# Four-layer image kernel on one Trainium2 core: whole residual tiles in the depthwise layer's transfers, and three setup blocks in another order

## The reference

```python
x = x + _L0_conv_ref(_gn(x), ...)   # attention, 8 heads of 48
x = x + _L1_conv_ref(_gn(x), ...)   # layer norm, diagonal complex state space, gated block
x = x + _L2_conv_ref(_gn(x), ...)   # depthwise convolutions
x = x + _L3_conv_ref(_gn(x), ...)   # RWKV mixing and a full 3x3 convolution

def _L2_conv_ref(x, w77, b77, w53, b53, w35, b35, w7w, w7h, w5w, w5h):
    bias = (b77 + b53 + b35)[None, :, None, None]
    out = dwconv(x, w77, 3, 3) + dwconv(x, w53, 2, 1) + dwconv(x, w35, 1, 2) \
        + dwconv(dwconv(x, w7w, 0, 3), w7h, 3, 0) + dwconv(dwconv(x, w5w, 0, 2), w5h, 2, 0) + bias
    return out
```

## Time and profile before

| | us |
|---|---|
| Median of 3 runs (lowest, highest) | 4443.89 (4439.7, 4444.58) |
| The profiled execution | 4441.98 |
| Its span | 4440.3 |
| Busy in the span: PE, DVE, ACT, POOL | 4000.5, 3117.9, 2279.3, 1358.7 |
| Mean busy share of the DMA engines over the span, largest queue | 21.7% |

### The profile page before, as it was taken

One profiled execution on the slowest core, in us unless ns is written; L12 is line 12 of the kernel. 1 busy time (PEld: TensorE's weight loads), 2 busy tenths in 40 slices (PEclk: granted clock), 3 DMA queues, 4 the chain that ended last, 5 costly groups with the idle time before them and its releaser, 6 DMA issues. The chain is left out here.

```text
span 4440.3 us, 55171 instructions
## 1 busy us (share of the span) xinstructions
PE 4000.5 (90%) x17483; PEld 2387.3 (54%) x17483; DVE 3117.9 (70%) x3175; ACT 2279.3 (51%) x3623; POOL 1358.7 (31%) x1008
## 2 busy tenths in 40 slices
PE   6999999999999999947999998565699999999999
PEld 5777777777777777723444443244244444444444
DVE  4757585757575757557777776425788888879878
ACT  2858585858585858533223332222445545544544
POOL 2858585858575758421111110110300000000000
PEclk8999999999999999968999999788799999999999
DMA  4323232323232323220111100458110110110110
GB/s 130 89 81 102 83 105 83 105 83 105 83 103 80 104 78 110 76 95 15 43 43 60 54 29 29 130 127 267 62 43 0 43 43 0 43 43 0 43 43 14
DMA packets 119503, 317.78 MB, mean 72 GB/s; under 512 B 49744, under 2 KB 51024, under 8 KB 109424
## 3 DMA queue, kind: packets, MB, share of 16 engines
q1 hardware_dynamic: 114000, 294.55, 21.7%
q0 software_dynamic: 2688, 12.42, 1.2%
q10 hardware_dynamic: 2592, 7.83, 0.6%
HBM read 207.64 MB, written 106.54 MB: 71 GB/s over the span
## 5 line engine op out<-in xcount | busy, mean ns | idle before, releaser
L404 POOL TENSOR_TENSOR probs_lo<-probs,probs_hi 128x512 fp32r<-128x512 f32 x848 | 1178.8, 1405 | 649.0 <-ACT probs L450 626.5
L510 DVE TENSOR_REDUCE maxima<-m_psum 128x1 fp32r<-128x1024 f32 x528 | 644.6, 1221 | 374.5 <-PE m_psum L678 373.6
L449 ACT ACTIVATE probs_hi<-s_psum 128x512 fp32r<-128x512 f32 x1024 | 613.2, 599 | 389.0 <-PE o_psum L707 226.6
L2317 PE MATMUL psum<-mixes,last_weights 128*128 128x512 f32 x1728 | 751.2, 593 | 0.0
L450 ACT ACTIVATE probs<-s_psum 128x512 f32<-128x512 f32 x1024 | 608.7, 594 | 0.0
L2317 PEld LDWEIGHTS psum<-mixes,last_weights 128*128 128x128 f32 x1728 | 327.9, 190 | 409.4 <-issue 409.4
L691 PE MATMUL s_psum<-q_all,k_hi 128*128 128x512 f32 x1026 | 426.7, 416 | 21.4 <-ACT probs L450 21.2
L707 PE MATMUL o_psum<-probs_lo,v 128*112 128x512 f32 x1024 | 412.4, 403 | 14.4 <-DVE probs_lo L590 7.6
L2324 PE MATMUL psum<-xp,last_weights 128*128 128x512 f32 x864 | 382.2, 596 | 25.6 <-DVEq L2201 13.3
L692 PE MATMUL s_psum<-q_all,k_lo 128*128 128x512 f32 x1026 | 404.4, 394 | 0.0
L702 PE MATMUL o_psum<-probs_hi,v 128*112 128x512 f32 x1024 | 403.6, 394 | 0.0
(11 more groups left out here) (322 smaller groups left out, 6130.4 us busy)
## 6 DMA issues: line engine op xcount, KB each, us to landing
xin<-in_x SPq DMA_DIRECT2D x17, 1536.0 KB, 7.5
xin<-x SPq DMA_DIRECT2D x17, 1536.0 KB, 6.7
k_hi<-k_rows_hi SPq DMA_DIRECT2D x134, 192.0 KB, 3.4
xres<-x SPq DMA_DIRECT2D x16, 1536.0 KB, 7.1
k_rows_hi<-stage_hi SPq DMA_DIRECT2D x54, 256.0 KB, 2.1
k_rows_lo<-stage_lo SPq DMA_DIRECT2D x54, 256.0 KB, 2.3
q_rows_hi<-stage_hi SPq DMA_DIRECT2D x52, 256.0 KB, 2.5
q_rows_lo<-stage_lo SPq DMA_DIRECT2D x52, 256.0 KB, 2.6
```

The source lines that it names most:

```text
L404: pool.tensor_tensor(probs_lo[:, u % RING, :], probs[:, u % RING, :], as_f32(probs_hi[:, u % RING, :]), ALU.subtract).then_inc(pool_low.ne ...
L449: nc.scalar.activation(probs_hi[:, u % RING, :], s_psum[:, u % 2, :], ACT.Exp, scale=SCALE)
L510: nc.vector.tensor_reduce(maxima[:, g % 2, tile:tile + 1], source, AX.X, ALU.max, negate=True).then_inc(rows_max.next(), 1)
L2317: ins = nc.tensor.matmul(bank, conv_w[:, t, down, factor, m * P:(m + 1) * P], mixes[:, factor, t, down:down + S, :].rearrange("p a b -> p ...
```

## The change

In layer 2 each residual load, each residual store and each band load is one transfer instead of four. The DRAM side of a residual transfer is written as blocks of 32 rows: 4 blocks at a distance of 3072 elements, 32 rows at a distance of 12288, 1024 elements. The SBUF side has 128 partitions. The band load reads 4 blocks, 32 rows, 1957 elements. In the setup of layer 2 the seven tap transfers go from ACT's queue to POOL's, the twelve bias transfers become three on POOL's, and the write of the padded taps goes from POOL's queue to SP's, ahead of load 4. ScalarE loads one table set at the start, and the sum of the biases comes after the ninth transpose. In layer 1 the tables are made in the main block at `i = -2`, one after the group norm's shift and one after `centre`. In layer 3 the weight transform is on VectorE, in four operations of which the third is fused.

```diff
@@ s5_layer, setup block @@
-                dve.wait_ge(counted.sem, counted.at(1))
-                do(V.tensor_copy(times, count))
-                for j in range(J):
-                    ... (ten operations for each table)
@@ s5_layer, ScalarE @@
+                if i == -2:
+                    for j in range(J):
+                        act.wait_ge(table_made.sem, table_made.at(j + 1))
+                        nc.scalar.activation(tables[:, :, j, :], tables[:, :, j, :], ACT.Sin, scale=TURN).then_inc(table_bent.next(), 1)
@@ s5_layer, VectorE @@
+            def table(j):
+                if j == 0:
+                    do(V.tensor_copy(times, count))
+                do(V.tensor_scalar(high, times, f_high[:, j:j + 1], None, ALU.mult))
+                do(V.tensor_scalar(whole, high, TO_ONE, TO_ONE, ALU.add, ALU.subtract))
+                do(V.tensor_tensor(high, high, whole, ALU.subtract))
+                do(V.scalar_tensor_tensor(high, times, f_low[:, j:j + 1], high, ALU.mult, ALU.add))
+                for n, quarter in enumerate((0.25, 0.0)):
+                    do(V.tensor_scalar(low, high, quarter, None, ALU.add))
+                    do(V.tensor_scalar(whole, low, TO_ONE, TO_ONE, ALU.add, ALU.subtract))
+                    last = V.tensor_tensor(tables[:, n, j, :], low, whole, ALU.subtract)
+                    ...
+                else:
+                    dve.wait_ge(table_bent.sem, table_bent.at(J))
+                if i == -2:
+                    table(0)
                 if here:
                     centre(norm2, y, averaged2, centred2, i)
                 ...
                     centre(norm1, f1[i % 2], averaged1, centred1, i + 2)
+                if i == -2:
+                    table(1)
@@ depthwise_layer, SP @@
-                for j in range(QUADS):
-                    sp.dma_start(res[j * S:(j + 1) * S, k % RING, :], x_quads[k // B, k % B, j]).then_inc(res_moved[k % RING], 16)
+                sp.dma_start(res[:, k % RING, :], x_quads[k // B, k % B]).then_inc(res_moved[k % RING], 16)
             for s in range(2 * B):
+                if s == RING:
+                    sp.wait_ge(tap_made.sem, tap_made.at(1))
+                    sp.dma_start(padded_dram[0:CT * CHANNELS]...).then_inc(tap_written, 16)
+                    sp.dma_start(padded_dram[CT * CHANNELS:]...).then_inc(tap_written, 16)
                 load(s)
-                for j in range(QUADS):
-                    sp.dma_start(out_quads[k // B, k % B, j], res[j * S:(j + 1) * S, k % RING, :]).then_inc(res_moved[k % RING], 16)
+                sp.dma_start(out_quads[k // B, k % B], res[:, k % RING, :]).then_inc(res_moved[k % RING], 16)
@@ depthwise_layer, POOL @@
+            for n, tile in taps.items():
+                pool.dma_start(...).then_inc(small_loaded, 16)
+            for n, tile in biases.items():
+                pool.dma_start(tile[:, :], w[n].rearrange("(r j t) -> j r t", j=QUADS, t=CT)).then_inc(vectors_loaded, 16)
-                for q in range(QUADS):
-                    target = bands[q * S:(q + 1) * S, g, :, :, :].rearrange("p a b c -> p (a b c)")[:, 0:READ]
-                    source = bass.AP(tensor=padded_dram.tensor, offset=padded_dram.offset + t * CHANNELS + (q * S + g * GROUP) * TAPS * ROW,
-                                     ap=[[1, S], [1, READ]])
-                    pool.dma_start(target, source).then_inc(band_loaded[n % 2], 16)
+                target = bands[:, g, :, :, :].rearrange("p a b c -> p (a b c)")[:, 0:READ]
+                source = bass.AP(tensor=padded_dram.tensor, offset=padded_dram.offset + t * CHANNELS + g * WINDOW,
+                                 ap=[[S * TAPS * ROW, QUADS], [1, S], [1, READ]])
+                pool.dma_start(target, source).then_inc(band_loaded[n % 2], 16)
@@ depthwise_layer, ScalarE @@
+            nc.scalar.preload_act_table_set("natural_log_exp_and_others")
@@ rwkv_layer, POOL @@
-            G.tensor_tensor(minus, g0, g2, ALU.add).then_inc(prepared.next(), 1)
-            ... (three more)
@@ rwkv_layer, VectorE @@
+            nc.vector.tensor_tensor(minus, g0, g2, ALU.add).then_inc(prepared.next(), 1)
+            nc.vector.tensor_tensor(minus, minus, g1, ALU.subtract).then_inc(prepared.next(), 1)
             dve.wait_ge(framed.sem, framed.at(11))
             ...
             shift(None)
+            nc.vector.scalar_tensor_tensor(g1, minus, 0.5, g1, ALU.mult, ALU.add).then_inc(prepared.next(), 1)
+            nc.vector.tensor_scalar(minus, minus, 0.5, None, ALU.mult).then_inc(prepared.next(), 1)
             for n in range(4):
                 mix(n, None)
```

More of the change, by code:

```diff
@@ L945, in _ @@
                         nc.scalar.copy(b_w[:, t, :, :].rearrange("p k q -> p (k q)"), psum[:, n % RING, :]).then_inc(kept.next(), 1)
-                for j, made in ((0, FIRST_TABLE), (1, SECOND_TABLE)):
-                    act.wait_ge(v.sem, v.at(made))
-                    nc.scalar.activation(tables[:, :, j, :], tables[:, :, j, :], ACT.Sin, scale=TURN).then_inc(s.next(), 1)
             @block.vector
@@ L1047, in s5_layer @@
         xin_free = signal("xin_free1")
+        table_step, table_made, table_bent = signal("table_step"), signal("table_made", J), signal("table_bent", J)
         step = signal("step1")
@@ L1224, in scale, with do @@
                     norm.vector_scale(at, half).then_inc(scaled.next(), 1)
+            def table(j):
+                V = nc.vector
+                def do(ins):
+                    ins.then_inc(table_step.next(), 1)
+                    dve.wait_ge(table_step.sem, table_step.now())
+                if j == 0:
[8 more added lines that the diff above has]
+                    last = V.tensor_tensor(tables[:, n, j, :], low, whole, ALU.subtract)
+                    if n == 0:
+                        do(last)
+                last.then_inc(table_made.next(), 1)
+                dve.wait_ge(table_made.sem, table_made.at(j + 1))
             def turn_in(i, half, between=None):
@@ L1573, in depthwise_layer @@
         STEPS = CT * B
-        SHIFT_MADE = 3
-        def quads(ap):
-            return ap.rearrange("(j r) n -> j r n", j=QUADS)
+        SHIFT_MADE = 4
+        VECTORS = len(biases) + len(last.VECTORS)
         def res_loaded(k):
-            return 2 * 16 * QUADS * (k // RING) + 16 * QUADS
+            return 2 * 16 * (k // RING) + 16
         def res_stored(k):
-            return 2 * 16 * QUADS * (k // RING + 1)
+            return 2 * 16 * (k // RING + 1)
         @block.sync
@@ L1622, in _ @@
                 pool.dma_start(last.cols[n][:, :], source.rearrange("(p t) -> p t", t=CT)).then_inc(vectors_loaded, 16)
[L1623 to L1627, removed]
+            pool.wait_ge(vectors_loaded, 16 * VECTORS)
             pool.wait_ge(tap_written, 32)
@@ L1663, in keep @@
                                    psum[:, n % 2 * QUADS + q, :, :].rearrange("p c n -> p (c n)")).then_inc(kept.next(), 1)
-            for n, tile in taps.items():
-                act.dma_start(tile[:, :, :, :].rearrange("p t a b -> p (t a b)"),
-                              w[n].rearrange("(p t) e a b -> p (t e a b)", t=CT)).then_inc(small_loaded, 16)
-            for n, tile in biases.items():
-                for j in range(QUADS):
-                    act.dma_start(tile[j * S:(j + 1) * S, :], w[n].rearrange("(r j t) -> j r t", j=QUADS, t=CT)[j]).then_inc(small_loaded, 16)
+            nc.scalar.preload_act_table_set("natural_log_exp_and_others")
             act.wait_ge(var_made.sem, var_made.at(1))
@@ L1674, in _ @@
             nc.scalar.activation(rstd[:, :], rstd[:, :], ACT.Exp, scale=-0.5).then_inc(rstd_made.next(), 1)
-            act.wait_ge(vectors_loaded, 16 * len(last.VECTORS))
-            nc.scalar.activation(last.fade[:, :], last.cols["w_param"][:, :], ACT.Exp).then_inc(fade_made.next(), 1)
             act.wait_ge(rstd_made.sem, rstd_made.at(1))
@@ L1680, in _ @@
                 normalise(s)
+                if s == B - 1:
+                    act.wait_ge(vectors_loaded, 16 * VECTORS)
+                    nc.scalar.activation(last.fade[:, :], last.cols["w_param"][:, :], ACT.Exp).then_inc(fade_made.next(), 1)
             for t in range(CT):
@@ L1726, in turn_back @@
                                        ALU.add, ALU.add).then_inc(back.next(), 1)
+            V.memset(padded[:, :, :, :], 0.0).then_inc(set_up.next(), 1)
             dve.wait_ge(grouped.sem, grouped.at(1))
@@ L1736, in _ @@
             assert set_up.count == SHIFT_MADE
-            V.memset(padded[:, :, :, :], 0.0).then_inc(set_up.next(), 1)
-            dve.wait_ge(small_loaded, 16 * (len(taps) + QUADS * len(biases)))
-            V.tensor_tensor(bias[:, :], biases["b77"][:, :], biases["b53"][:, :], ALU.add).then_inc(set_up.next(), 1)
-            settled()
-            V.tensor_tensor(bias[:, :], bias[:, :], biases["b35"][:, :], ALU.add).then_inc(set_up.next(), 1)
+            dve.wait_ge(small_loaded, 16 * len(taps))
```

(6 more changed lines are left out.)

25 lines of the change are left out of this document (13 added, 12 removed).

## The result

The changed kernel takes 4578.45 us (median of 4, 4572.28 to 4590.87) against 4444.24 us (4 runs): 1.0304 times as long, 95% interval 1.0291 to 1.0317. The forecast was 4556, slower.

The account below looks back on a forecast made before the run. Transfers bound the end of layer 2, VectorE layer 1's prologue, short chains the starts of layers 2 and 3. +134 - 4 - 13.3 - 5 = +112 on 4442, plus 1.9 for the median: 4556; range 4395 to 4630.

Parts of the forecast that it names:

- The turn-back: End of layer 2: merged residual transfers fall to the same four DMA engines and queue, 261 us instead of 126.7, +134.
- The packets: Sign at the end of layer 2: 132 packets for each merged transfer (128 and 4 closings) instead of 192.
- (a): Merged transfers are dealt to all 16 DMA engines, so the kernel is faster, 4399 us (4380 to 4425); chance 0.24.
- (b): Four engines for each merged transfer, but another four each time, so that four run at once: 4422 us; chance 0.05.
- The start of layer 2: Setup chain and transposes run earlier, first convolution matmul still awaits its band: -4 us (-6.5 to +2).
- A merged band load dealt to four engines: Layer 2's first band: 32 rows, 9.4 to 17.6 us, and 2 for landing, so there at 2852 to 2861.
- The second step: Layer 2, SP's queue: input loads 4 to 7 wait for the taps, up to 8 us later, still ahead of their transposes.
- Later bands are loaded four groups ahead and stay hidden: Layer 2: band loads after the first cost no time; no size given.
- Layer 3: Weight transform moved from POOL to VectorE at the layer's start: -13.3 us, at worst -10.
- Both stalls: Layer 3's start: two tiny VectorE operations of 7.40 and 7.52 us beside POOL's fall to 0.2 each, -7.2 and -7.4.
- Layer 1: Main block starts 18.1 us earlier, table work partly fills VectorE's idle times, POOL contention adds up to 10.1: -5 us.
- lie beside the matmuls: Layer 1: two Sine activations, 1.91 us each, run beside the matmuls that fill the first state; the rotation must wait for them.

## Why the prediction was right, and where not

**The turn-back: right in mechanism and size.** +134 was forecast, +128.2 came. The row cost was taken as 0.165 us near the low end and was 0.159; the stretch took 254.9 us and not 261. The packets (132 for each merged transfer) and the share of about a quarter came as described; VectorE's waits were 164.7 us, where 180 were named. The rule of the Trainium skill, "DMA: Bandwidth & Descriptors", section "Why a DMA increments its semaphore by 16 and not by 1", on the number of engines agrees with the runs for counts of 32, 4 and 2 (closings of 16, 4 and 2). That transfers of a hardware queue use the same engines each time agrees as well (25.5 and 12.8%); that these are the lowest-numbered no trace shows. Rivals (a) and (b) are refuted, (a) by the closings, (b) by the share of 25.5%, which would be more if transfers ran on different engines.

**The start of layer 2: wrong.** -4 was forecast and +23.8 came. Two steps failed. The first is "A merged band load dealt to four engines is 32 rows, 9.4 to 17.6 us, and 2 for landing". Nearly alone a whole band takes 17.0 us, inside these bounds, but the first one landed 33 us after its issue. Input tiles run on all sixteen engines beside it, and its rows took 0.70 us in the mean instead of 0.37. What I priced was a queue with little else in it. POOL issues two bands at once, but up to eight of their rows were in flight, so the second was mostly not on the engines of the first.

The second step is that loads 4 to 7 go out "up to 8 us later, still ahead of their transposes of 1.8 us each", with no price for input tiles that run beside whole bands. Their eighth transpose ends 15.2 us later than before (46.3 against 31.1). With the bands in parts it is 38.7: half of the delay remains, because SP holds the loads for the taps (24.1 when POOL writes them). The other half, 7.6 us, is the whole bands. This step alone would have made the first matmul at least 13.4 of the 15.3 us late.

From the first matmul to the turn-back another 8.5 us were lost (141.4 against 132.9). TensorE's wait of 5.21 us names the cause, ScalarE's first copy behind its sixteenth input tile, and by the third group nearly all of the delay stands. "Later bands are loaded four groups ahead and stay hidden" held: each band from the second on had landed before its matmuls, though POOL waited 61.1 us for bands ahead of its next issues. Without whole bands and without SP's wait for the taps, the first matmul comes at 29.8 and not 38.7, of which 4.5 us are left at the turn-back in single executions. Why input tiles land so late beside whole bands is argued only: a tile has rows on all sixteen engines and is whole when the busiest is done.

**Layer 3: right.** -13.3 forecast, -11.8 measured. Both stalls went as said, and the additions took 3.76 us each as against 3.9.

**Layer 1: right in sign, the contention too large.** -5 forecast, -6.3 measured. The delay of the prologue's last scaling is 10.5 us against the forecast 13.8 (from the shift to the scaling 31.2 instead of 20.7). POOL and VectorE hold each other up, but share the cost: eight additions of POOL lengthened VectorE's table work by 7.6 us and POOL's own by 3.3, where I put all 10.1 on VectorE. All table operations beside POOL were slowed alike, also those that read one tile. One step failed: that the Sine activations "lie beside the matmuls". VectorE waits 4.00 us for ScalarE at the next image's shift (1966.57), behind both activations and the table loads around them, where it waited 0.50; at the first use of the tables 1.1 us of this are left.

**The sum.** 4556 was near 4578 because the large term was right. The 22 us between them are the 28 us by which the start of layer 2 was missed, less the 6 that the turn-back was cheaper; the other terms cancel within 2 us. The sign and most of the size rest on the mechanism; that the time is no farther off is in part luck, since the steps that failed stood beside a term of 128 us. The lower end of the range, called the middle of (a), is 4395 where (a) was worked out as 4399; nothing hangs on it.

## What to carry to other kernels

Before transfers are merged, write down the access pattern of both sides. Here the DRAM side decided: with an outermost count of 32 a transfer used all sixteen engines, with 4 and 2 only four and two, and on SP's queue always the same ones. Other counts, and a small count on the SBUF side, were not run. The signs in a trace are closings of k and not 16 for each transfer and a DMA share of k sixteenths under a long wait.

And price a transfer by the load around it, in both directions: a whole band that lands in 17 us nearly alone takes 33 beside input tiles, and the input tiles come late beside it, which by itself would have cost most of the 15.3 us at the first matmul. If an engine's program puts all loads of a stage ahead of the first work on results, the last load holds that work up.

## What the runs showed of the hardware that was not expected

On POOL's queue a transfer with an outermost count of 4 brings many 4-byte packets: 400 for a whole band of 128 rows (4800 over 12 bands, and 4032 packets more on that queue than with plain parts) and 448 for one in four parts of that form, against 64 for plain parts. Both counts come out as 16 closings and, for each of the 12 engines without rows, one packet for each row of a busy engine: 16 + 12 x 32 = 400, and 4 x (16 + 12 x 8) = 448. That fits two counts and was not tested further. On SP's queue the same form had only its 4 closings. What these packets are for is open.
